# A macaron transformer block on one core: new order around the projections, five score banks at the end, seven row maxima a head taken by way of ScalarE and GpSimd

## The chip, the cores and the metric

The kernel runs on one core of one Trainium2 chip. The metric is the device time of one launch in microseconds (us), the median of the runs. Engines are named as the profile names them: PE is TensorE (matmuls), PEld its weight loads, DVE is VectorE, ACT is ScalarE, POOL is GpSimd, SP is SyncE (here it only issues DMAs). Each engine works through its own list in order and waits on semaphores for the others.

## The reference

Input x is 4096 tokens by 256 features. The block is feed-forward, attention, feed-forward:

```
x = x + 0.5 * ffn(layernorm(x))
x = x + attn(layernorm(x))
x = x + 0.5 * ffn(layernorm(x))

ffn(x):  h = x @ W_exp + b_exp ; h = butterfly(h, up) ; h = gelu(h + up_bias)
         h = butterfly(h, down) ; y = h @ W_con + b_con + down_bias
attn(x): 16 heads of 16 features, causal
         Q, K, V = x @ WQ, x @ WK, x @ WV
         probs = softmax(where(causal, Q K^T / sqrt(16), -inf))
         sum over heads of (probs @ V) @ WO
```

Everything is float32. The two butterflies are linear, so the kernel folds them into the two weight matrices once at the start.

## The kernel before

**Stages.** The start folds the weights (to about 77 us of the span). Then a loop over t = 0 to 8 runs the first feed-forward on tile t (512 tokens) and, beside it, the Q, K and V projections of tile t-1 (77 to 368 us). Then the attention runs head by head (368 to 1716 us), and at last the second feed-forward with the output projection (1716 to 1930 us).

**The loop over t.** For each tile PE runs eight hidden blocks h0 to h7 (6 matmuls each, `up_block`, L1119), of which `H_AHEAD` = 6 stand ahead of the four Q/K projections (`qk` w = 0 to 3, 6 matmuls each, L1222). The transposes of the normalized tile t-1 (XN2A, in OA) stand before block `H_AHEAD - 2`, so after four blocks. After h7 come the transposes of XN (tile t+1), the V projection (L1143) and four y blocks (L1149). Hidden blocks and qk blocks alternate over two PSUM banks (`TURNS`), so each waits until the block two places before it has been read out: `gelu_done` by ACT for h, `parts_done` for qk (ACT copies the high part, L684, DVE subtracts for the low part, `low_parts`, L935). SP stores each of the four parts to DRAM (L476), w = 0, 1 being q and w = 2, 3 being k, and loads head 0's slices back (`load_q` L437/L438, `load_k` L430/L431). DVE adds the residual of each y block (L923), takes its statistics (L774), and after the last one computes 1/sigma (L795 to L813) and normalizes into XN2A (L827). Beside the y blocks PE already computes scores for the first row maxima of head 0 (L1169) and DVE reduces them (L955 with a causal mask, L959 without); the list for block b is `beside_y`, and the ones of the last block stand on DVE before its residual.

**Attention.** The softmax needs its row maxima before the exponentials. So each score matrix is computed twice. One pass has queries on the partitions: 128 queries by 512 keys per unit (`maximum`, L1169 on PE), whose row maximum DVE takes straight from PSUM (L959, 512 elements; L955 on the diagonal). The other has keys on the partitions (`scores`, L1277), from which ACT makes exponentials (L729) into one of 8 buffers, POOL zeroes the causal triangle (L587), and PE multiplies with V (`values`, L1293). The maximum of each row is subtracted in the second pass by two extra rows of the operands (`split_step` L906 to L915 and `load_m` L449).

A head has 144 units (`UNITS`: 36 pairs (j, c) of query tile j and key tile c, times 4 blocks), in the order j = 5, 4, 3, 2, 1, 0, 6, 7. Work is issued in groups of 3 units: on PE three pairs "scores(u), maximum(u + 92)" and then the values of earlier units. The maxima run 92 units (`MX_AHEAD`) ahead of the scores. In the last head the maxima end 92 units before the scores do (`MX_UNITS` = 2212 of 2304 units); from there scores run alone. PSUM has 3 banks for scores (`S_BANKS`), so scores(u) wait for the exponential of u-3; 4 banks for maxima (`MAX_BANKS`), so maximum(u) waits until DVE has reduced u-4; one bank for the sums of values. The two score passes use different row halves of the PE array and run beside each other.

In the last head, groups 24, 25, 26 and 28 carry one output-projection block each, and group 37 the transposes of the second feed-forward's first tile.

The order of all engines is written out by hand in program order; nothing is scheduled by a tool.

## Time and profile before

| what | value |
|---|---|
| runs | 1930.58, 1930.83, 1930.94 us; median 1930.83 |
| profiled execution, its own time | 1931.87 us |
| its span (first to last instruction) | 1930.1 us |
| TensorE clock granted, mean | 0.996 of full speed |
| PE busy | 1884.0 us (98%) |
| DVE busy | 1653.3 us (86%) |
| ACT busy | 1374.1 us (71%) |
| POOL busy | 319.5 us (17%) |

How to read it: matmuls are pipelined and their modelled ends overlap, so PE counts as busy while one drains even if the next has not been issued; "98%" is not a full PE. The duration that a row gives for one instruction includes its latency; the distance between two in a row (the pitch) is shorter. The waits between engines tell more than the shares.

### The profile page before, as it was taken

How to read it: one execution, taken by the hardware profiler on the slowest of the kernel's cores; microseconds unless marked ns; L12 is line 12 of the kernel's file. 1: busy time of each engine (PE TensorE's matmuls, PEld its weight loads, DVE VectorE, ACT ScalarE, POOL GpSimd, SP SyncE). 2: the span in 40 equal slices, each digit the busy share in tenths (PEclk: the TensorE clock that was granted, in tenths of full speed). 3: DMA queues.
4: the chain of work that ended last, by engine and by line, in shares of the span. 5: the costliest groups of instructions: out<-in, count | busy, mean ns of one | idle time of the engine just before them, and what ended most of it. 6: DMA issues, size and time to landing. Idle time of an engine off the chain costs nothing.

```text
span 1930.1 us, 62111 instructions
## 1 busy us (share of the span) xinstructions
PE 1884.0 (98%) x24312; PEld 1326.1 (69%) x24312; DVE 1653.3 (86%) x3631; ACT 1374.1 (71%) x2778; POOL 319.5 (17%) x738
## 2 busy tenths in 40 slices
PE   4999999999999999999999999999999999999999
PEld 3788778666666666666666666666666666679998
DVE  7746566799999999999999999999999999746763
ACT  5412222488888888888888888888888888875443
POOL 4100000011111111111111111111111111135444
PEclk8999999999999999999999999999999999999999
DMA  7111122212111111211111121211112111102210
GB/s 202 48 56 52 53 77 78 67 48 56 42 50 46 48 44 40 55 42 51 47 46 45 41 55 41 51 46 47 46 41 55 41 49 35 55 26 66 66 44 23
DMA packets 82836, 102.40 MB, mean 53 GB/s; under 512 B 16752, under 2 KB 45168, under 8 KB 82544
## 3 DMA queue, kind: packets, MB, share of 16 engines
q1 hardware_dynamic: 81920, 98.03, 18.0%
q8 instruction: 193, 3.16, 0.7%
q14 instruction: 99, 0.81, 0.1%
q10 hardware_dynamic: 624, 0.40, 0.1%
HBM read 68.46 MB, written 29.36 MB: 51 GB/s over the span
## 4 chain that ended last, share of the span: by engine, by line
PE 91%; DVE 6%; ACT 1%; issue 1%; POOL 0%; DMA 0%; ACTq 0%; POOLq 0%; DVEq 0%
PE PS L1293 31%; PE PS L1277 29%; PE PS L1169 10%; PE PS L1149 7%; PE PS L1119 6%; PE PS L1341 5%; PE PS L1222 1%; PE PS L1143 1%; PE PS L1085 1%; DVE MXP L959 1%; DVE BNS L774 1%; DVE OA L827 1%; DVE OA L935 1%; POOL QT L609 0%; DVE OA L839 0%
## 5 line engine op out<-in xcount | busy, mean ns | idle before, releaser
L729 ACT ACTIVATE PG<-PS 128x512 f32<-128x512 f32 (+3 forms) x2304 | 1137.0, 562 | 161.5 <-PE PS L1277 136.4
L959 DVE TENSOR_REDUCE MXP<-PS 128x1 f32<-128x512 f32 x1792 | 1088.2, 682 | 14.0 <-PE PS L1169 13.1
L1169 PE MATMUL PS<-KT,QT 48*128 48x512 f32 (+5 forms) x2304 | 783.1, 432 | 3.5 <-DVE MXP L959 2.2
L1277 PE MATMUL PS<-QT,KT 50*128 50x512 f32 (+3 forms) x2304 | 727.2, 421 | 0.3
L1293 PE MATMUL PS<-PG,VH 128*17 128x128 f32 x16896 | 651.1, 275 | 0.1
L1293 PEld LDWEIGHTS PS<-PG,VH 128*17 128x17 f32 x16896 | 432.7, 97 | 197.4 <-issue 181.7
L1277 PEld LDWEIGHTS PS<-QT,KT 50*128 50x128 f32 x2304 | 360.0, 184 | 267.7 <-ACT PG L729 193.9
L1169 PEld LDWEIGHTS PS<-KT,QT 48*128 48x128 f32 (+1 forms) x2304 | 371.9, 184 | 24.9 <-DVE MXP L959 13.3
L587 POOL TENSOR_SCALAR_AFFINE_SELECT PG<-PG 128x128 f32<-128x128 f32 x512 | 145.1, 292 | 964.3 <-ACT PG L729 953.9
L955 DVE CUSTOM_DVE_ANT_0 PS<-PS,MASK 128x128 f32<-128x128 f32 (+3 forms) x512 | 241.6, 514 | 38.0 <-PE PS L1169 37.3
L658 ACT ACTIVATE PG<-PS,GB 128x512 f32<-128x512 f32 x128 | 90.3, 706 | 166.4 <-PE PS L1119 166.4
L923 DVE TENSOR_TENSOR X<-PS,X 128x256 f32<-128x256 f32 x96 | 40.5, 423 | 136.8 <-PE PS L1149 91.4
L1149 PE MATMUL PS<-MD,PG 128*128 128x256 f32 x512 | 117.8, 381 | 2.2 <-DVE X L923 1.4
L1149 PEld LDWEIGHTS PS<-MD,PG 128*128 128x128 f32 x512 | 96.2, 190 | 15.9 <-DVE X L923 1.8
L1119 PE MATMUL PS<-XTH,MU 128*128 128x512 f32 x256 | 103.3, 404 | 3.4 <-DVE MUL L893 1.6
L1119 PE MATMUL PS<-XTH,MUL 128*128 128x512 f32 x256 | 100.9, 394 | 0.0
L1119 PE MATMUL PS<-XTL,MU 128*128 128x512 f32 x256 | 100.6, 393 | 0.0
L609 POOL TENSOR_TENSOR QT<-PG,KT 128x512 fp32r<-128x512 f32 x64 | 85.8, 1383 | 82.5 <-ACT PG L658 82.5
L566 POOL TENSOR_TENSOR X<-X,OB 128x1024 f32<-128x1024 f32 x16 | 38.3, 2393 | 277.5 <-DVE XN L827 251.8
L578 POOL COPY VH<-V 128x68 f32<-128x68 f32 x128 | 30.3, 240 | 270.0 <-PE PS L1293 193.5
L1341 PE MATMUL PS<-W,KT 128*128 128x256 f32 x256 | 74.1, 289 | 0.6 <-POOL QT L609 0.6
L955 DVE DVE_READ_ACCUMULATOR2_ANT MXP<- 128x1 f32 x512 | 73.6, 144 | 0.0
(113 smaller groups left out, 1209.5 us busy)
## 6 DMA issues: line engine op xcount, KB each, us to landing
QT<-q_parts SPq DMA_DIRECT2D x256, 64.0 KB
KT<-k_parts SPq DMA_DIRECT2D x256, 64.0 KB
q_parts<-OA SPq DMA_DIRECT2D x16, 512.0 KB, 2.8
QT<-q_parts SPq DMA_DIRECT2D x256, 32.0 KB
k_parts<-OA SPq DMA_DIRECT2D x16, 512.0 KB, 4.9
KT<-k_parts SPq DMA_DIRECT2D x256, 32.0 KB
o_parts<-OS SPq DMA_DIRECT2D x128, 64.0 KB
OA<-o_parts SPq DMA_DIRECT2D x32, 256.0 KB
```

The lines of the kernel that those rows point to most:

```text
L587: nc.gpsimd.affine_select(out=tri, in_=tri, compare_op=ALU.is_ge, fill=0.0, base=0, pattern=[[1, P]], channel_multiplier=-1).then_inc(mask ...
L609: nc.gpsimd.tensor_tensor(GL[:, b, :].bitcast(f32r), G[:, b, :], GH[:, b, :], ALU.subtract).then_inc(gl_rdy, 1)
L658: nc.scalar.activation(G[:, b, :], src, ACT.Gelu, bias=GB[:, b:b + 1]).then_inc(gelu_done, 1)
L729: nc.scalar.activation(PB[u % P_BUFFERS][:, q0:TILE], bank(u % S_BANKS)[:, q0:TILE], ACT.Exp, scale=1.0 / DH ** 0.5).then_inc(exp_done, 1)
L955: nc.vector.tensor_tensor_reduce(out=s, in0=s, in1=MASK[:, 3 * P - qs * P:3 * P - qs * P + w], scale=1.0, scalar=-3e38, op0=ALU.add, op1=A ...
L959: nc.vector.tensor_reduce(dst, bank(b), AX.X, ALU.max).then_inc(mx_red, 1)
L1119: last = mm(dst, w[:, k, b * P:(b + 1) * P].bitcast(f32r), x[:, k, :].bitcast(f32r), start=(k == 0 and x is XTH and w is MU), stop=(k == D ...
L1149: last = mm(y_bank(b, y), lhs[:, k, b * P:(b + 1) * P], rhs[:, k, :], start=(k == 0), stop=(k == nk - 1))
L1169: mm(bank(b, w), q[0:rows, (BT * place(j) + qs) * P:(BT * place(j) + qs + 1) * P].bitcast(f32r), k[0:rows, c * TILE:c * TILE + w].bitcast( ...
L1277: mm(bank(u % S_BANKS)[:, q0:TILE], kt[0:SM, kb * P:(kb + 1) * P].bitcast(f32r), qt[0:SM, place(j) * TILE + q0:(place(j) + 1) * TILE].bitc ...
L1293: last = mm(O_SUM[qs * Q32:qs * Q32 + DV, :], VH[:, c * BT + kb, :], PB[u % P_BUFFERS][:, qs * P:(qs + 1) * P], start=(j == c and kb == 0) ...
L1341: last = mm(y_bank(b, y), g[:, i, cols].bitcast(f32r), w[:, i, :].bitcast(f32r), start=(i == 0 and w is MDH and g is GH), stop=(i == HB - ...
```

## The change

Five edits in one:

1. `H_AHEAD` goes from 6 to 7. Seven hidden blocks stand ahead of the projections, one behind, and the transposes of XN2A stand after five blocks.
2. On DVE, of the last y block's list the items from the third on (`beside[2:]`) move behind the normalization into XN2A; `normalize(XN, t + 1)` moves ahead of `low_parts`.
3. The four parts are computed and stored in the order q low half, k low half, q high half, k high half (`PART_AT`). SP loads q for head 0 after the third store and k after the fourth, waiting for the second store instead of the third; `load_m(0)` follows the third store instead of the second.
4. From unit 2212 on, scores use five banks (`LAST_BANKS`): the three and two of the maxima's.
5. For items m of a head with m % 12 == 1 off the diagonal (seven: 13, 37, 49, 97, 109, 121, 133), from unit 36 on, ACT copies the 512 scores from PSUM to SBUF (`copy_maxima`), POOL folds the two halves of 256 into their maximum with three operations (subtract, clamp at zero, add; `fold`), and DVE reduces the 256 that are left three groups later (`final_maximum`). The count of `mx_red` no longer follows the item's number, so waits go by a table (`RED_N`).

The first place is DVE's list in the loop over t, in the iteration t = 4, from the last y block to the low parts (OA is the normalized tile t-1, X from PS are the transposed parts). Before:

```order
L959 TENSOR_REDUCE MXP<-PS 128x1 x4
L923 TENSOR_TENSOR X<-PS,X 128x256
L774 BN_STATS BNS<-X 128x6
L795 TENSOR_TENSOR LN<-BNS 128x4
...
L827 TENSOR_SCALAR OA<-X,MEAN,RSTD 128x256 x4
L867 CAST X<-PS 128x1024
L869 TENSOR_TENSOR X<-PS,X 128x1024
L935 TENSOR_TENSOR OA<-PS,OA 128x512 x4
L827 TENSOR_SCALAR XN<-X,MEAN,RSTD 128x256 x4
```

The same place after the change:

```order
L1032 TENSOR_REDUCE MXP<-PS 128x1 x2
L996 TENSOR_TENSOR X<-PS,X 128x256
L847 BN_STATS BNS<-X 128x6
L868 TENSOR_TENSOR LN<-BNS 128x4
...
L900 TENSOR_SCALAR OA<-X,MEAN,RSTD 128x256 x4
L1032 TENSOR_REDUCE MXP<-PS 128x1 x2
L940 CAST X<-PS 128x1024
L942 TENSOR_TENSOR X<-PS,X 128x1024
L900 TENSOR_SCALAR XN<-X,MEAN,RSTD 128x256 x4
L1008 TENSOR_TENSOR OA<-PS,OA 128x512 x4
```

Two reductions have moved from ahead of the residual to behind the normalization, and XN's normalization from behind the low parts to ahead of them.

The second place is SP's list at the last tile's parts (MT holds the split maxima that `load_m(0)` brings into the score operands). Before:

```order
L476 DMA q_parts<-OA 128x2x512 x2
L449 DMA QT<-MT 2x16x32 x4
L437 DMA QT<-q_parts 32x1x512
L438 DMA QT<-q_parts 16x512
L437 DMA QT<-q_parts 32x1x512
L438 DMA QT<-q_parts 16x512
L476 DMA k_parts<-OA 128x2x512 x2
```

After:

```order
L508 DMA q_parts<-OA 128x2x512
L508 DMA k_parts<-OA 128x2x512
L508 DMA q_parts<-OA 128x2x512
L480 DMA QT<-MT 2x16x32 x4
L468 DMA QT<-q_parts 32x1x512
```

The four small loads from MT now stand behind three stores, not two.

The third place is ACT's list in a head, around its diagonal pair (5, 5) (PG from PS are exponentials, OS the sums of values). Before:

```order
L729 ACTIVATE PG<-PS 128x384
L729 ACTIVATE PG<-PS 128x256
L738 ACTIVATE OS<-PS 128x128
L729 ACTIVATE PG<-PS 128x128
L729 ACTIVATE PG<-PS 128x512 x21
```

After:

```order
L788 ACTIVATE PG<-PS 128x384
L788 ACTIVATE PG<-PS 128x256
L808 ACTIVATE OS<-PS 128x128
L788 ACTIVATE PG<-PS 128x128
L788 ACTIVATE PG<-PS 128x512 x2
L800 ACTIVATE OA<-PS 128x512
L788 ACTIVATE PG<-PS 128x512 x12
L800 ACTIVATE OA<-PS 128x512
L788 ACTIVATE PG<-PS 128x512 x7
```

A copy of 512 (OA from PS) now stands among the exponentials once every 12 units.

The diff, cut to its core:

```diff
+PART_AT = (0, 2, 1, 3)
+FINAL_BEHIND = 3
+C_BUFFERS = 6
+FOLD_WIDTHS = (256,)
+FOLD_STEPS = 3 * len(FOLD_WIDTHS) - 1
-H_AHEAD = 6
+H_AHEAD = 7
+COPIED = frozenset(m for m in range(NU) if m % 12 == 1)
...
+        def copied(u):
+            _, _, j, c, _ = unit(max_item(u))
+            return NU // 4 <= u < MX_UNITS and j != c and max_item(u) % NU in COPIED
+        def finals_in(g):
+            return [u for u in items_in(g - FINAL_BEHIND) if copied(u)] if g >= FINAL_BEHIND else []
+        LAST_BANKS = [(MX_UNITS + i) % S_BANKS for i in range(S_BANKS)] + [MAX_BANKS[3], MAX_BANKS[2]]
+        def s_bank(u):
+            return u % S_BANKS if u < MX_UNITS else LAST_BANKS[(u - MX_UNITS) % len(LAST_BANKS)]
...
             for t in range(NT):
+                for w in range(3):
+                    store_part(t, w)
+                if t == NT - 1:
+                    load_m(0)
...
+                sp.wait_ge(parts_out[0], 16 * (t + 2))
+                load_q(NQ, 0, t, ld_nq[t])
+                load_q(CQ, 0, t, ld_cq[t])
+                store_part(t, 3)
+                sp.wait_ge(parts_out[1], 16 * (t + 2))
                 load_k(NK, 0, t, ld_nk[t])
                 load_k(CK, 0, t, ld_ck[t])
...
+            def fold(u):
+                n = COPY_N[u]
+                c = COPY[n % C_BUFFERS]
+                pool.wait_ge(mx_copied, n + 1)
...
+                    nc.gpsimd.tensor_tensor(d, d, c[:, 0:w], ALU.subtract).then_inc(fold_step, 1)
+                    pool.wait_ge(fold_step, done + 1)
+                    nc.gpsimd.tensor_scalar(d, d, 0.0, None, ALU.max).then_inc(fold_step, 1)
+                    pool.wait_ge(fold_step, done + 2)
+                    last = nc.gpsimd.tensor_tensor(c[:, 0:w], d, c[:, 0:w], ALU.add)
...
+                last.then_inc(mx_folded, 1)
             for g in range(GROUP_N):
                 for u in group_units(g):
                     mask(u)
+                for u in items_in(g):
+                    if copied(u):
+                        fold(u)
...
+            def copy_maxima(u):
...
+                if n >= C_BUFFERS:
+                    act.wait_ge(mx_red, RED_N[COPIES[n - C_BUFFERS]])
+                act.wait_ge(mx_ps, max_item(u) + 1)
+                nc.scalar.activation(COPY[n % C_BUFFERS], bank(mx_bank(u)), ACT.Copy).then_inc(mx_copied, 1)
...
                     normalize(XN2A, t - 1, seq_p(t - 2) + 1 if t > 1 else None)
+                    for item in beside[2:]:
+                        maximum0(*item)
...
+                if t + 1 < NT:
+                    normalize(XN, t + 1, seq_f(t) + 1)
                 if t:
                     low_parts(t - 1, pair(late, "qk") if t < NT else ())
-                if t + 1 < NT:
-                    normalize(XN, t + 1, seq_f(t) + 1)
...
+                        beside = beside_y(late, soon, t, b)
+                        residual_block(t, t, b, beside[:2] if b == BT - 1 else beside)
...
+            def final_maximum(u):
+                _, n, j, c, qs = unit(max_item(u))
+                dve.wait_ge(mx_folded, COPY_N[u] + 1)
+                nc.vector.tensor_reduce(MXP[...], COPY[...][:, 0:FOLD_WIDTHS[-1]], AX.X, ALU.max).then_inc(mx_red, 1)
             for g in range(GROUP_N):
+                for u in finals_in(g):
+                    final_maximum(u)
...
+                elif before >= 0 and copied(before):
+                    pe.wait_ge(mx_copied, COPY_N[before] + 1)
...
-                if u >= S_BANKS:
+                if u == MX_UNITS + S_BANKS:
+                    pe.wait_ge(mx_red, H * NMX + FREE_MX)
+                elif u >= MX_UNITS + len(LAST_BANKS):
+                    pe.wait_ge(exp_done, u - len(LAST_BANKS) + 1)
+                elif u >= S_BANKS and s_bank(u) < S_BANKS:
                     pe.wait_ge(exp_done, u - S_BANKS + 1)
```

## Rows read from the trace of the kernel before

**Rows 1.** Busy time in one stretch of the attention; columns: stretch, length, each engine (instructions).
```profile
800.00:1000.00 200.00, 200.00 (x3194) 128.58 (x3192) 197.06 (x435) 173.72 (x362) 25.15 (x92) 1.00 0.18 47
```
**Rows 2.** The chain in order of time: start, length, what; one piece per head.
```profile
1109.84 1.22 PE PS L1293 x28
1278.03 1.22 PE PS L1293 x28
```
**Rows 3.** Groups by line, whole trace: busy us, mean ns | idle before, releaser.
```profile
L959 DVE TENSOR_REDUCE MXP<-PS 128x1 f32<-128x512 f32 x1792 | 1088.2, 682 | 14.0 <-PE PS L1169 13.1
L906 DVE TENSOR_REDUCE NEGM<-MXP 128x16 f32<-128x128 f32 x32 | 9.0, 281 | 0.1
L684 ACT ACTIVATE OA<-PS 128x512 fp32r<-128x512 f32 x32 | 19.1, 598 | 33.9 <-PE PS L1222 33.9
L587 POOL TENSOR_SCALAR_AFFINE_SELECT PG<-PG 128x128 f32<-128x128 f32 x512 | 145.1, 292 | 964.3 <-ACT PG L729 953.9 <-issue 0.6
L314 POOL TENSOR_TENSOR V<-V 128x256 f32<-128x256 f32 x1 | 0.7, 724 | 0.1
```
**Rows 4.** Timelines of attention: DVE, then PE's value phases and ACT without DVE's wait.
```profile
1039.81 10.85 DVE L959 TENSOR_REDUCE MXP<-PS 128x1 f32<-128x512 f32 x18
1101.48 0.85 PE L1293 MATMUL PS<-PG,VH 128*17 128x128 f32 x24
1104.92 0.85 PE L1293 MATMUL PS<-PG,VH 128*17 128x128 f32 x24
1102.86 3.25 ACT L729 ACTIVATE PG<-PS 128x512 f32<-128x512 f32 x6 [0.17 <-PE PS L1277]
```
**Rows 5.** Who waited for whom, whole trace: total us, times, longest.
```profile
PEld PS L1085 <- DVE OA L827: 11.8, 8, 1.7
PEld PS L1119 <- DVE OA L935: 4.8, 14, 0.5
PEld PS L1169 <- issue: 3.0, 5, 1.1
```
**Rows 6.** Timelines of DVE and PE at t = 4, and PE at t = 8.
```profile
187.68 1.29 DVE L959 TENSOR_REDUCE MXP<-PS 128x1 f32<-128x512 f32 x2 [0.90 <-PE PS L1169]
193.24 1.38 DVE L827 TENSOR_SCALAR OA<-X,MEAN,RSTD 128x256 f32<-128x256 f32 x4 [0.15 <-DVE RSTD L813]
194.67 1.09 PE L1085 MATMUL PS<-ident,OA 128*128 128x128 f32 x8 [1.31 <-DVE OA L827]
352.71 1.09 PE L1085 MATMUL PS<-ident,OA 128*128 128x128 f32 x8 [1.47 <-DVE OA L827]
```
**Rows 7.** The chain in order of time at t = 3: two hidden blocks.
```profile
155.46 2.75 PE PS L1119 x12
```
**Rows 8.** Timelines of SP and PE at t = 4: k loads and first maxima.
```profile
206.94 0.93 SPq L476 DMA_DIRECT2D k_parts<-OA  x2
211.64 0.61 SPq L430 DMA_DIRECT2D KT<-k_parts  x1
217.35 0.47 PE L1169 MATMUL PS<-KT,QT 128*128 128x128 f32 x2 [0.68 <-issue]
```
**Rows 9.** Timelines of SP, DVE and PE where the attention begins.
```profile
363.56 2.66 SPq L449 DMA_DIRECT2D QT<-MT  x4
364.21 0.69 DVE L935 TENSOR_TENSOR OA<-PS,OA 128x512 fp32r<-128x512 f32 x1 [1.09 <-ACT OA L684]
367.67 0.49 PE L1277 MATMUL PS<-QT,KT 50*128 50x512 f32 x1
```
**Rows 10.** Timelines of PE and ACT in the last head, scores alone.
```profile
1706.28 1.25 PE L1277 MATMUL PS<-QT,KT 50*128 50x512 f32 x3
1708.24 0.76 PE L1277 MATMUL PS<-QT,KT 50*128 50x512 f32 x3
1709.71 1.25 PE L1277 MATMUL PS<-QT,KT 50*128 50x512 f32 x3
1708.84 3.05 ACT L729 ACTIVATE PG<-PS 128x512 f32<-128x512 f32 x6 [0.39 <-PE PS L1277]
```

More of the change, by code:

```diff
@@ L187, in wide @@
             return oa[:, i * DK * TILE:(i + 1) * DK * TILE].rearrange("p (k t) -> p k t", k=DK)
+        COPY = [oa[:, 5 * DK * TILE + i * TILE:5 * DK * TILE + (i + 1) * TILE] for i in range(C_BUFFERS)]
         OT, SUMS, XT2B = [wide(i) for i in range(2)], [wide(2 + i) for i in range(2)], wide(4)
@@ L375, in max_item, with items_in @@
             return u + MX_AHEAD
+        def copied(u):
+            _, _, j, c, _ = unit(max_item(u))
+            return NU // 4 <= u < MX_UNITS and j != c and max_item(u) % NU in COPIED
+        def items_in(g):
+            return [u for u in group_units(g) if u < MX_UNITS]
+        def finals_in(g):
+            return [u for u in items_in(g - FINAL_BEHIND) if copied(u)] if g >= FINAL_BEHIND else []
+        COPY_N = {u: n for n, u in enumerate(u for u in range(MX_UNITS) if copied(u))}
+        COPIES = list(COPY_N)
+        RED_N = {}
+        for g in range(GROUP_N):
+            for u in finals_in(g) + [u for u in items_in(g) if not copied(u)]:
+                RED_N[u] = MX_AHEAD + FREE_MX + len(RED_N) + 1
         def split_items(i):
@@ L708, in _ @@
                     mix_a_side(1, (2,), range(4, 8))
+                    gelus(0, 0, range(6, H_AHEAD))
                 elif t < NT:
@@ L742, in _ @@
                     exponential(u)
+                for u in items_in(g):
+                    if copied(u):
+                        copy_maxima(u)
                 for u in VALUES_IN[g]:
@@ L1215, in _ @@
                         turn_free("qk", u)
-                        cols = slice((w % 2) * P, (w % 2 + 1) * P)
+                        part = PART_AT[w]
+                        cols = slice((part % 2) * P, (part % 2 + 1) * P)
                         for k in range(DK):
@@ L1219, in _ @@
                                 pe.wait_ge(xt_rdy, seq_p(t - 1) + 1)
-                            high, low = WH[:, w // 2, k, cols], WL[:, w // 2, k, cols]
+                            high, low = WH[:, part // 2, k, cols], WL[:, part // 2, k, cols]
                             for i, (wt, x) in enumerate(((high, X2H), (high, X2L), (low, X2H))):
```

49 lines of the change are left out of this document (28 added, 21 removed).

## The prediction

> **What bounds the kernel now.** I read four views. The page's busy shares first: they name PE (98%), but a draining matmul counts as busy, so they don't decide. Then the busy time per stretch: in 200 us of attention DVE works 197.1 us, ACT 173.7, POOL 25.2 [rows 1]. The groups by line say the same: DVE waited only 14.0 us in front of its 1792 reductions of 512 scores [rows 3]. So from 368 to 1660 us DVE is the tightest engine. The chain gives the period of a head, (1278.03 - 1109.84) / 2 = 84.10 us [rows 2], that is 1.75 us for each of 48 groups of three units.
>
> Then the timelines. DVE takes 18 reductions in 10.85 us; without the last one's tail that is 0.598 us each, 1.79 us for three [rows 4]. Where DVE is ahead (after diagonal maxima, which are cheaper), PE's value phases start at 1101.48 and, two groups on, at 1104.92, which is 1.72 us a group [rows 4]. This is a ring: scores(u) wait for the exponential of u-3, and ACT makes six in 3.25 us and waits again [rows 4]. Its own pitch is about 0.49 us (six in 3.05 less a tail of 0.1) [rows 10], so of 3.44 us ACT has 0.48 idle, 0.24 a group. So DVE's bound is above the ring's by only 0.07 us a group. That is the number that limits what the maxima edit can bring.
>
> In the loop over t the waits are PE's: 11.8 us for the normalized tile before the transposes, 8 times; 4.8 us for low parts before hidden blocks, 14 times; 3.0 us of "issue" before first maxima, 5 times [rows 5]. In the last head alone PE goes in pairs of groups, 1706.28 to 1709.71, 3.43 us for six units, while ACT needs 2.95 [rows 10].
>
> **The loop over t: the wait before the transposes.** At t = 4 two reductions take DVE 1.2 us ahead of the last residual, and the normalization ends at 194.62, after which PE starts, having idled 1.31 us, up to 1.7 in its weight queue [rows 5, 6]. The edit takes the 1.2 us out of this chain and puts one more hidden block in front of the transposes; two blocks last 2.75 us, one 1.38 [rows 7]. Together 2.6 us against at most 1.7: the wait goes. Up to t = 3 the last y block has no third item, and the block alone does it, save some 0.2 at t = 1. The wait at t = 8 (1.47, about 1.7 in the queue) stays, for no block is there to fill it [rows 6]. So 11.8 - 1.7 - 0.2 = 9.9 us. What is late next: the moved reductions start where the transposes are still running, and the cast needs these, so they hide; after the transposes two blocks follow as before, so the first projection finds its operands as early as now.
>
> **Normalizing XN earlier** puts 1.4 us of DVE in front of the low parts. DVE idles there, since ACT has to read out a projection that PE has yet to run (before the third low part of the last tile it idles 1.09 us [rows 9]). I cost it at nothing; without cover it would be up to 1.4 us for seven tiles, 10 us.
>
> **One hidden block behind the projections instead of two.** Of the 14 waits for low parts the longest is 0.5; if h6's seven are all that long, 1.3 us is left for h7's seven, 0.17 each [rows 5]. h7 now waits for the third, and the smaller wait goes: 7 x 0.17 = 1.2 us of the 4.8.
>
> **Order of the parts.** At t = 4 the third and fourth part's stores are issued from 206.94 on, k's loads only at 211.64, when the third has landed, and PE stands at 217.35 for them [rows 8]. Now the k half that head 0 needs is stored second, so it has landed by the time of the fourth store, and its loads follow that one at about 208, 3.5 us earlier, against maxima that come 1.4 us earlier. So the 3.0 us of "issue" go [rows 5].
>
> **Against it: the first scores.** `load_m(0)` stood behind the second store and was issued from 363.56 to 366.22; the first scores start at 367.67 without a wait in PE's row, so at most 1.4 us after the last load's issue. The third low part ends at 364.90, and with its store's issue (0.4) ahead the loads now start at about 365.3, 1.8 us later [rows 9]. A landing of 1.2 us leaves 0.2 to 0.3 in hand, so the first scores start some 1.5 us later, once (bounds 0.4 and 1.8).
>
> Sum of the stage: -9.9 - 1.2 - 3.0 + 1.5 = -12.6 us. Ends: -14 and, with the normalization uncovered and the last wait doubled, -1.
>
> **Five banks in the last head.** ACT's rhythm there has 0.39 us idle per six exponentials, and PE's phase of three scores lasts 1.2 us when it waits for an exponential and 0.7 when it doesn't (group periods 1.96 and 1.47) [rows 10]. With five banks scores run two further ahead and the long phase goes: the floor is PE's 1.47 or ACT's 3 x 0.49 = 1.48 us a group instead of 1.72. 31 groups, of which some 24 full: 12 pairs x 0.47 = 5.6 us. Off goes about 1 us: the wait for the last reduction before the first borrowed bank, and the last split's loads, which are on time by under 1 us now and will be overtaken. So -4.6; ends -5.7 and -1.5.
>
> **The seven maxima a head.** There are 4 in the first head, 7 in each of 14, 4 in the last: 106. DVE: a reduction of 128 has a mean of 281 ns, one of 512 of 682 [rows 3], so one of 256 is 281 + 401/3 = 415 ns, and each copied item frees 682 - 415 = 267 ns. 106 x 0.267 = 28.3 us is the most that the edit can give. ACT: a copy of 512 from PSUM has a mean of 598 ns [rows 3], a pitch of 0.49 like the exponentials. It stands behind the third exponential of a group, where 0.24 us is idle on average; 0.25 is pushed into the next group. In four of the seven places that group's first exponential is the 128-wide one of a diagonal, some 0.23 us shorter, which leaves hardly anything. So of twelve units: DVE 12 x 0.598 = 7.18 before, 6.91 after; the ring 4 x 1.72 = 6.88 plus 0.02 in four places and about 0.22 in three. The larger counts: gains of 0.25 in four places and 0.08 in three, 1.24 us a head. One of the three (item 49, issued beside unit 101) lies in a stretch where PE already runs at the ring's pace: nothing to gain, 0.1 to 0.2 to lose. That leaves 1.1 us a head, 1.1 x 106/7 = -16.7 us. Ends: -28.3, and +26 if each copy pushed the ring by the full 0.25 and DVE's relief bought nothing.
>
> POOL: three operations of 256. A two-input one takes 724 ns, the one-input one at least what 128 columns of the causal mask take, 292, and at most 724 [rows 3]: 1.74 to 2.17 us, plus waits between them, about 2.2. Masks queue behind it on POOL, and the values wait for them; but after each copied unit the next diagonal unit is at least three units away, and the values of that one are a group behind. DVE asks for the folded half three groups later. From the third exponential of the group to there are 7 units of 0.58 plus DVE's lag of about 0.5, so 4.6 us, less 1.1 for the copy: 3.5 us for a fold of 2.2. Hidden.
>
> A page speaks against folding on POOL. The masked reductions (PSUM and one SBUF input) and the plain ones are as long beside a mask on POOL as without, which is what the near-constant 0.598 says [rows 4]. "SBUF — State Buffer" of the Trainium skill (section "SBUF: two separate sides") states that a VectorE operation with two SBUF inputs, or one in a two-port mode, and a GpSimd operation lock each other out for a whole instruction. By that rule only the casts and subtractions of the splits could collide, and they stand in other groups than the folds: the sum stays, and only if the lock reached further is there the rival E. No run here yet shows a fold.
>
> **Sum.** -12.6 - 4.6 - 16.7 = -33.9 us, from the profiled execution's 1931.9 (span 1930.1, 1.8 around it): 1898.0. That execution is 1.0 above the median of the runs, so 1897. The second feed-forward is untouched.
>
> **Rivals.**
> A, the forecast: 1897, by itself 1890 to 1905. Chance 0.55.
> B, the ring takes all of DVE's relief: ACT's copies cost what they free. For it speaks the margin of 0.07 us a group; against it the four places beside a short exponential. 1930.8 - 12.6 - 4.6 = 1914. Chance 0.17.
> C, the ring has more give than its unhindered pace shows, and all 28.3 us come: 1885. For it: DVE's waits for PE are small everywhere. Chance 0.12.
> D, the stage keeps its waits, moved to the low parts behind the early normalization or to the y blocks: only a few us of 12.6: about 1907. The three waits were all short and late in a chain, which speaks against it. Chance 0.08.
> E, DVE's reduction of the fold, or a masked one beside it, is blocked for the length of a POOL operation, 0.72: 0.2 to 0.3 us for each of 106, 1920 to 1925. Chance 0.03.
> F, slower: ACT is late for the ring after every copy. Its price is 0.25 x 106 = +26.5, less 17.2 from the other two parts: 1940. It turns the sign from 0.16 us net loss per copied item on. Against it: only every fourth group has a copy, and ACT has 0.48 us idle in two. A fold longer than 3.5 us would do the same by way of DVE. Chance 0.05.
>
> The range 1883 to 1916 holds A, B, C and D but for their edges. What a measurement of this kernel can tell from no change is 0.2%, 3.9 us: all but F is faster by more, so faster 0.93, within 0.2% 0.02, slower 0.05.
>
> **What the profile after would show.** PE's wait for the normalized tile at 1.7 us in all instead of 11.8, "issue" before the first maxima gone, periods of t shorter by 1 to 2.5 us, the first scores waiting for loads after the V projection. Heads of about 83.0 us instead of 84.1; DVE's idle time in the attention up, from 3 us in 200 to 4 or more; the reductions of 256 near 415 ns; POOL some 230 us more busy; ACT at 90% instead of 87. The last 92 units in about 50 us instead of 55. Wrong would be: heads at 84 us or more with PE's scores waiting for exponentials after copies (B, F), DVE idle in front of the folded reductions (F's second way), waits in front of the low parts (D).

## The result, and the profile of the changed kernel

| | before | after |
|---|---|---|
| median of the runs, us | 1930.88 (1930.58 to 1932.65, 4 runs) | 1913.53 (1912.39 to 1914.80, 4 runs) |
| ratio | | 0.9906, 95% interval 0.9893 to 0.9918 |
| profiled execution / span, us | 1931.9 / 1930.1 | 1913.25 / 1911.5 |

The kernel is 17.4 us faster by the medians. The forecast was 1897. Sign and range held; the size is half of what was worked out. Cut at the same events in both traces, the spans differ by 18.6 us:

| stretch | before, us | after, us | change | forecast |
|---|---|---|---|---|
| start to the first set of XN2A transposes (t = 1) | 78.46 | 76.66 | -1.8 | the stage as a whole: -12.6 |
| from there to the set at t = 8 | 274.25 | 263.92 | -10.3 | |
| from there to the first exponential | 15.49 | 17.04 | +1.5 | |
| head 0 | 83.92 | 85.82 | +1.9 | -0.6 |
| heads 1 to 14, mean of one | 84.13 | 83.82 | -0.31, in all -4.4 | -1.1, in all -15.4 |
| head 15 up to unit 2212 | 30.49 | 30.04 | -0.4 | -0.6 |
| last 92 units | 54.87 | 49.78 | -5.1 | -4.6 |
| rest | 214.76 | 214.78 | 0 | 0 |

The forecast of the profiled execution was 1898.0 and it took 1913.25. Of these 15.3 us the heads from 1 on hold 11.2, head 0 holds 2.5 and the stage 2.0; the last 92 units came out 0.5 better than forecast.

The first row is not the work of the change. The first set of transposes starts at 76.7 to 80.2 us in the eleven kernels of this document that have the stage as it is after the change, the changed kernel among them, and the scatter is there before the loop over t begins. The second row is: 263.9 to 266.5 us in the same eleven, 7.8 to 10.3 below the kernel before.

**The stage.** The waits of the kernel after, as in [rows 5] (engine and line, who was waited for: total us, times, longest; L1170 is L1085 of before, L1204 is L1119, L1254 is L1169):

```profile
PEld PS L1204 <- DVE OA L1008: 3.6, 7, 0.5
PEld PS L1170 <- DVE OA L900: 2.0, 2, 1.7
PEld PS L1254 <- issue: 1.1, 2, 0.7
```

11.8 us of waits for the normalized tile are 2.0, of which 1.7 is the one at t = 8; the seven short waits for low parts are gone, 1.2 us; of the 3.0 us of "issue" 1.1 are left in this execution. These are waits of PE's weight queue, and what they cost is less. At t = 4 before the change, where PE's row shows 1.31 us idle [rows 6], the queue waited 1.73, but from the start of the last matmul ahead to the first transpose it took 1.70 us where 0.23 is the distance without a wait:

```profile
192.97 0.39 PE L1119 MATMUL PS<-XTH,MUL 128*128 128x512 f32 x1
194.67 0.86 PEld L1085 LDWEIGHTS PS<-ident,OA 128*128 128x128 f32 x8 [1.73 <-DVE OA L827]
```

Over t = 1 to 7 these distances sum to 9.9 us before and 1.6 after, so the wait's going gave 8.3 us, not 9.8. At t = 4 the two timelines of [rows 6] are now these (start, length, what):

```profile
186.37 1.38 DVE L900 TENSOR_SCALAR OA<-X,MEAN,RSTD 128x256 f32<-128x256 f32 x4 [0.15 <-DVE RSTD L886]
187.67 1.28 DVE L1032 TENSOR_REDUCE MXP<-PS 128x1 f32<-128x512 f32 x2
```
```profile
188.90 0.39 PE L1204 MATMUL PS<-XTH,MUL 128*128 128x512 f32 x1
189.13 1.03 PE L1170 MATMUL PS<-ident,OA 128*128 128x128 f32 x8
```

The tile is ready at 187.67 and PE reaches its transposes at 189.13 without a wait: 1.4 us in hand. The last k part and its loads come in one go now. Before, the first of them was issued at 211.64 [rows 8], 4.2 us after the transposes of XN had started (207.48); here those start at 200.51, and the load follows 2.0 us later:

```profile
201.96 0.52 SPq L508 DMA_DIRECT2D k_parts<-OA  x1
202.52 0.61 SPq L461 DMA_DIRECT2D KT<-k_parts  x1
```

**The first scores, and what they brought with them.** SP, then PE, where the attention begins, against [rows 9]:

```profile
352.78 0.36 SPq L508 DMA_DIRECT2D q_parts<-OA  x1
353.19 2.65 SPq L480 DMA_DIRECT2D QT<-MT  x4
```
```profile
354.73 0.87 PE L1228 MATMUL PS<-W,X 128*128 128x256 f32 x6
357.12 0.46 PE L1369 MATMUL PS<-QT,KT 50*128 50x512 f32 x1 [1.52 <-DMA QT<-MT]
```

PE stands 1.5 us for the loads of the maxima, which are issued behind the third store; their last issue ends at 355.84 and the scores start 1.28 us later. That was the forecast. What was not: PE had been busy up to that gap, and from 358.2 us on the granted clock is down at the lower level (columns: PE, PEld, DVE, ACT, POOL busy, then PEclk, DMA share, GB/s):

```profile
354.00:358.00 4.00, 2.48 (x20) 1.94 (x18) 0.66 (x3) 1.54 (x4) 1.49 (x8) 1.00 0.34 115
358.00:365.00 7.00, 6.81 (x53) 3.92 (x54) 5.22 (x9) 3.71 (x9) 1.10 (x4) 0.51 0.42 126
365.00:372.00 7.00, 7.00 (x125) 4.35 (x122) 6.86 (x13) 6.30 (x12) 0.00 (x0) 1.00 0.35 74
```

0.51 is the 1.2 GHz level, for nearly the whole of 7 us in which PE is busy for 6.81. The kernel with the loads early, below, has neither the gap nor this stretch, and not head 0's +1.9 us either.

**The heads.** The chain in order of time, one piece a head, of which two ten heads apart stand here (start, length, what), and the busy time of the stretch that [rows 1] shows for before:

```profile
679.60 1.22 PE PS L1385 x28
1517.67 1.22 PE PS L1385 x28
```
```profile
800.00:1000.00 200.00, 200.00 (x3198) 128.02 (x3194) 195.45 (x437) 181.50 (x383) 64.81 (x150) 1.00 0.18 48
```

(1517.67 - 679.60) / 10 = 83.81 us a head. ACT has risen from 173.7 to 181.5 us of 200, POOL from 25 to 65, DVE has fallen only from 197.1 to 195.5. The groups by line (busy us, mean ns | idle before):

```profile
L1032 DVE TENSOR_REDUCE MXP<-PS 128x1 f32<-128x512 f32 x1686 | 1041.5, 681 | 23.7 <-PE PS L1254 16.8
L637 POOL TENSOR_SCALAR OA<-OA 128x256 f32<-128x256 f32 x106 | 89.5, 845 | 9.3
L635 POOL TENSOR_TENSOR OA<-OA 128x256 f32<-128x256 f32 x106 | 77.6, 732 | 290.9 <-ACT OA L800 290.9
L639 POOL TENSOR_TENSOR OA<-OA 128x256 f32<-128x256 f32 x106 | 77.5, 731 | 8.8
L800 ACT ACTIVATE OA<-PS 128x512 f32<-128x512 f32 x106 | 64.7, 611 | 0.0
L1102 DVE TENSOR_REDUCE MXP<-OA 128x1 f32<-128x256 f32 x106 | 43.4, 409 | 0.0
```

The reduction of a folded half takes 409 ns (forecast 415), the copy 611 (598), so each copied item does free 0.27 us of DVE and costs ACT no more than was put down. DVE never waits for a folded half (idle 0.0 before L1102). What DVE got, it idles away in part. The 14.0 us in front of the plain reductions before [rows 3] and the 23.7 now are of the whole trace, and 13.8 and 12.2 of them lie in the loop over t; from 372 to 1640 us, in the attention, it is 0.2 us before and 11.4 now. In heads 1 to 14 together DVE's idle time has risen from 19.3 to 31.7 us, and they are 4.4 us shorter. The unit prices were right, and the worth of a freed 0.27 us was not.

**The last head.** ACT in [rows 10] idled 0.39 us per six exponentials. Now, in the head's last stretch of scores:

```profile
1684.87 11.87 ACT L788 ACTIVATE PG<-PS 128x512 f32<-128x512 f32 x24 [0.39 <-PE PS L1369]
```

24 exponentials in 11.87 us without a gap among them: 0.49 us each, which is ACT's own pitch.

### The profile page after: what moved, and what is told of

It reads as the page before. It is cut to its first block, busy times and chain, and to the rows that moved or that the text cites. A ratio compares the mean times of both kernels' runs of the same rounds, so it can differ in the third digit from the quotient of the medians.

```text
span 1911.5 us, 62638 instructions
## 1 busy us (share of the span) xinstructions
PE 1869.8 (98%) x24312; PEld 1310.3 (69%) x24312; DVE 1634.6 (86%) x3631; ACT 1416.7 (74%) x2884; POOL 562.6 (29%) x1056
## 4 chain that ended last, share of the span: by engine, by line
PE 94%; DVE 3%; ACT 1%; DMA 1%; POOL 0%; issue 0%; SPq 0%; POOLq 0%; ACTq 0%; DVEq 0%
PE PS L1385 31%; PE PS L1369 30%; PE PS L1254 9%; PE PS L1204 8%; PE PS L1234 7%; PE PS L1433 5%; PE PS L1310 1%; PE PS L1170 1%; PE PS L1228 1%; DVE OA L1008 1%; DMA PG<-w_exp_t 1%; ACT OA L698 0%; POOL QT L667 0%; DVE OA L912 0%; ACT OA L742 0%
## 5 line engine op out<-in xcount | busy, mean ns | idle before, releaser
L1032 DVE TENSOR_REDUCE MXP<-PS 128x1 f32<-128x512 f32 x1686 | 1041.5, 681 | 23.7 <-PE PS L1254 16.8
L1254 PE MATMUL PS<-KT,QT 48*128 48x512 f32 (+5 forms) x2304 | 782.6, 430 | 2.7 <-DVE MXP L1032 2.2
L1254 PEld LDWEIGHTS PS<-KT,QT 48*128 48x128 f32 (+1 forms) x2304 | 373.9, 185 | 22.4 <-DVE MXP L1032 8.9
L635 POOL TENSOR_TENSOR OA<-OA 128x256 f32<-128x256 f32 x106 | 77.6, 732 | 290.9 <-ACT OA L800 290.9
L667 POOL TENSOR_TENSOR QT<-PG,KT 128x512 fp32r<-128x512 f32 x64 | 85.8, 1382 | 80.7 <-ACT PG L716 80.7
L1204 PE MATMUL PS<-XTH,MU 128*128 128x512 f32 x256 | 102.2, 399 | 3.5 <-DVE MUL L966 1.6
L1204 PE MATMUL PS<-XTH,MUL 128*128 128x512 f32 x256 | 100.0, 391 | 0.0
L1204 PE MATMUL PS<-XTL,MU 128*128 128x512 f32 x256 | 99.8, 390 | 0.0
L637 POOL TENSOR_SCALAR OA<-OA 128x256 f32<-128x256 f32 x106 | 89.5, 845 | 9.3
```

Source lines behind the costliest of these rows:

```text
L637: nc.gpsimd.tensor_scalar(d, d, 0.0, None, ALU.max).then_inc(fold_step, 1)
L1032: nc.vector.tensor_reduce(dst, bank(b), AX.X, ALU.max).then_inc(mx_red, 1)
L1204: last = mm(dst, w[:, k, b * P:(b + 1) * P].bitcast(f32r), x[:, k, :].bitcast(f32r), start=(k == 0 and x is XTH and w is MU), stop=(k == D ...
L1254: mm(bank(b, w), q[0:rows, (BT * place(j) + qs) * P:(BT * place(j) + qs + 1) * P].bitcast(f32r), k[0:rows, c * TILE:c * TILE + w].bitcast( ...
```

## The experiments

Twelve kernels ran, each timed in several rounds beside the kernel before on the same chip. Ratios are to the kernel before, with 95% intervals. "Head" is the mean of heads 1 to 14, from the exponentials' starts in the profile. Where it matters, units are counted within a head (0 to 143), as are the items of the maxima.

### No copies

```diff
-COPIED = frozenset(m for m in range(NU) if m % 12 == 1)
+COPIED = frozenset()
```

> The changed kernel with no item copied: all maxima are reduced by VectorE from PSUM, the rest of the change stays. What the copies are worth by themselves, all else equal. Theory R (the ring of scores and exponentials over three banks sets the pace of the attention almost everywhere, so VectorE's relief turns into idle time): heads back at 84.08 us, time 1913.5 + 4.8 = 1918. Theory of the prediction (1.1 us a head): 1930. A theory S (the copies cost as much as they bring, and the small gain per head comes from elsewhere): 1913 to 1915.

Measured: 1921.53 us (1918.94 to 1923.24), ratio 0.9946 (0.9931 to 0.9961). Head 84.19 us, last 92 units 49.65. So five banks give their 5 us without any copy, the heads without copies are those of before, and seven copies are worth 84.19 - 83.82 = 0.37 us a head. The medians of the two kernels differ by 8.0 us, their profiles by 8.6, but 3.9 of those lie ahead of the attention, where nothing was edited; so the worth of the copies is read from the heads here, and from the heads below.

### Half reductions: VectorE relieved as far as it goes

No copies, and each unmasked reduction in the attention reads 256 of its 512 scores (half of the keys are left out of those maxima).

```diff
-nc.vector.tensor_reduce(dst, bank(b), AX.X, ALU.max)
+nc.vector.tensor_reduce(dst, bank(b)[:, 0:256], AX.X, ALU.max)
```

> No item copied, and every unmasked row maximum takes only the first 256 of its 512 columns (the other half of the keys is left out of the maxima). VectorE is freed of 0.27 us in each of 112 units a head, 30 us a head, and ScalarE and GpSimd have nothing added: this shows the pace of the ring without VectorE and without copies. Theory R: heads of about 82.5 to 83.3 us, barely under the changed kernel's 83.75, time 1900 to 1910. If VectorE were the bound and only ScalarE's copies had eaten the gain: heads under 82 us, time under 1890.

Measured: 1889.61 us (1889.07 to 1890.56), ratio 0.9782 (0.9768 to 0.9797); head 82.27 us. The group and the stretch:

```profile
L1032 DVE TENSOR_REDUCE MXP<-PS 128x1 f32<-128x256 f32 x1792 | 658.2, 418 | 321.0 <-PE PS L1254 320.6
```
```profile
800.00:1000.00 200.00, 200.00 (x3270) 124.61 (x3268) 137.41 (x449) 177.83 (x371) 26.69 (x97) 1.00 0.18 46
```

DVE idles 321 us in front of its reductions, and a head is only 1.92 us shorter than with none of this. That is about all that relief of DVE can bring here: 15 heads x 1.9 = 29 us for some 60 us of idle DVE in each 200. The forecast's pace of the ring, 1.72 us for each of 48 groups, makes 82.56 us and was nearly right (82.27). So the ring was sized well; how fast one gets down to it was not.

### Copies without their use

Seven copies a head of the same size on ScalarE, read from SBUF; nothing is folded and DVE reduces every item from PSUM.

```diff
-nc.scalar.activation(COPY[n % C_BUFFERS], bank(mx_bank(u)), ACT.Copy).then_inc(mx_copied, 1)
+nc.scalar.activation(COPY[n % C_BUFFERS], MD[:, 0:2, :].rearrange("p a b -> p (a b)"), ACT.Copy).then_inc(mx_copied, 1)
...
-                for u in finals_in(g):
-                    final_maximum(u)
-                    if u < MX_UNITS and not copied(u):
+                    if u < MX_UNITS:
```

> Nothing is copied from the maxima, VectorE reduces all of them from PSUM and GpSimd folds none, but ScalarE makes a copy of 512 (from the folded down weights in SBUF into a spare buffer) at the same 106 places. ScalarE's burden without any relief. Theory R says that ScalarE is in the ring: each copy costs 0.02 to 0.25 us, 0.5 to 1 us a head on top of 84.1, against the kernel without copies +7 to +15 us. If ScalarE's idle time swallows the copies: within 2 us of the kernel without copies, about 1918.

Measured: 1924.07 us (1923.01 to 1926.35), ratio 0.9962 (0.9948 to 0.9976); head 84.41. Copies alone cost 0.22 us a head. That is not 0.03 each: units 100 to 107, where item 49 is copied, take 4.91 us here and 4.67 without copies, so this one copy costs 0.24, the 0.25 that rival F needed, and the other six together nothing (beside the copy of item 133 units 40 to 43 are 0.17 us longer, and 44 to 47 give 0.15 back). With the relief they are 0.37 ahead of none, so the relief, with the other release of the copied items' banks, is worth 0.59 us of the 7 x 0.27 = 1.87 that it frees.

### No fold

POOL folds nothing; DVE reduces the first 256 of the copy (half of the keys of the copied items are left out).

```diff
-                    if copied(u):
-                        fold(u)
...
-                dve.wait_ge(mx_folded, COPY_N[u] + 1)
+                dve.wait_ge(mx_copied, COPY_N[u] + 1)
```

> The changed kernel, but GpSimd folds nothing: VectorE reduces the first 256 columns of the copy as soon as ScalarE has made it (the other half of those keys is left out of these 106 maxima). GpSimd's part alone is taken away. Theory R: no difference, 1912 to 1914. If the fold of 2.5 us (its clamp takes 845 ns and not the 292 to 724 that were assumed) held up masks or VectorE's last reduction: faster by up to 0.2 us a copy, 1895 to 1908.

Measured: 1914.36 us (1913.72 to 1914.87), ratio 0.9910 (0.9895 to 0.9925); head 83.84 against 83.82. The fold, 732 + 845 + 731 ns on POOL, is hidden to the last tenth, and nothing on DVE is shorter for its absence (L1102 has 409 ns in both). Rival E is out, and F by way of late folds.

### The maxima's loads back behind the second store

```diff
 for w in range(3):
     store_part(t, w)
-if t == NT - 1:
-    load_m(0)
+    if t == NT - 1 and w == 1:
+        load_m(0)
```

> The changed kernel with the first loads of the split maxima back behind the second store. In the changed kernel PE waits 1.7 us in front of the first scores, and its granted clock is then at the lower level from 358 to 365 us of the span. Theory: the wait goes, and with it the stretch at the lower clock, which costs head 0 some 1.9 us: 1913.5 - 3.4 = 1910. If the stretch at the lower clock has nothing to do with the wait: only 1.5 us, 1912.

Measured: 1911.41 us (1909.69 to 1913.60), ratio 0.9900 (0.9885 to 0.9914): 2.1 us below the kernel after in another set of runs, with intervals that overlap, so the times alone don't carry it. The profiles do: head 0 takes 83.58 us instead of 85.82, and PE has the full clock in the stretch where it had half:

```profile
354.00:358.00 4.00, 4.00 (x22) 3.42 (x23) 1.66 (x3) 1.99 (x4) 0.00 (x0) 1.00 0.71 264
358.00:365.00 7.00, 6.74 (x72) 4.89 (x72) 5.03 (x10) 5.13 (x13) 2.48 (x12) 1.00 0.56 178
```

Over all profiles: the five with three score banks and the loads behind the third store have 3.4 or 6.8 us of low clock just behind the first scores, the seven with the loads behind the second (before among them) have none after the first exponential. In full-reduction kernels head 0 then takes 84.9 to 86.0 us in the one case (84.9 and 85.1 behind 3.4 us, 85.8 and 86.0 behind 6.8) and 83.4 to 83.9 in the other. A piece of 3.4 us at the lower level 11 to 13 us ahead of the first exponential is another matter: nine of the fourteen kernels have it, the one before the change too, with and without the gap.

### The same, and item 49 not copied

```diff
-COPIED = frozenset(m for m in range(NU) if m % 12 == 1)
+COPIED = frozenset(m for m in range(NU) if m % 12 == 1 and m not in (49,))
```

> As the kernel before it (loads early), and item 49 of a head is no longer copied, so six instead of seven a head. Theory R: at that place ScalarE's copy pushes the ring and VectorE's relief buys nothing (the pairs (6, 2) and (6, 1) are 0.23 + 0.04 us longer than before the change, 0.07 comes back at (6, 0)): 0.2 us a head less, 15 times, 1907. If each copy is worth the same seventh of the gain: +0.7, 1911.

Measured: 1907.38 us (1906.82 to 1908.79), ratio 0.9880 (0.9863 to 0.9896), the shortest of all with the whole computation. Head 83.57 against 83.84 with seven: the seventh copy costs 0.27 us a head where the forecast had put a loss of 0.1 to 0.2. It is the sharpest sign that a copy's worth is a matter of its place, and the kernel with copies alone shows what this one costs: units 100 to 107 take 4.90 us with all seven, 4.91 with copies alone, 4.69 here and 4.67 without any. ScalarE's time is lost there and DVE's relief brings nothing.

### Four score banks, three for the maxima

With copies and without, loads early in both; the last 92 units keep five banks.

```diff
-S_BANKS = 3
+S_BANKS = 4
-MAX_BANKS = (4, 5, 7, 3)
+MAX_BANKS = (4, 5, 7)
```

> Loads early, all seven copies, and one PSUM bank moved from the maxima (three left) to the scores (four) for the whole attention. Scores of u then wait for the exponential of u-4. Theory R: the ring over three banks is what limits, so four free it, and VectorE, with its relief, becomes the bound: heads of about 82.5, time 1890 to 1900. If the fourth bank of the maxima is what keeps VectorE fed: PE waits for VectorE more, heads of 84 to 86, time 1915 to 1940.

> As the kernel with four score banks, without any copy. Theory R: VectorE is then the bound in nearly every group, 83.0 us of work a head plus some waits, about the same as now, 84: time 1912 to 1918, so that the copies are worth 10 to 20 us in this form where they are worth under 5 in the other. If the number of score banks does not matter: the difference between the two stays under 5.

Measured: 2022.74 us, ratio 1.0475 (1.0459 to 1.0490), head 91.08 with copies; 2004.83 us, 1.0385 (1.0369 to 1.0400), head 89.91 without. So the score ring doesn't set the pace by itself: a bank added there and taken from the maxima costs 6 to 7 us a head. The waits of PE for the maxima's banks, without copies, show why (49 waits with 13.3 us of before, whole trace, have become these):

```profile
PEld PS L1254 <- DVE MXP L1032: 101.0, 369, 2.7
```

PE takes scores and maxima in one order, so a maxima bank that isn't free holds up the scores as well. And here seven copies lose 1.17 us a head, relief and all, where with four maxima banks they win 0.37. A copied item keeps its bank until ACT comes to it, and the trace with copies shows PE waiting for that, in each of heads 1 to 14 once, behind item 49's place, for 0.47 us (whole trace):

```profile
PEld PS L1254 <- ACT OA L800: 7.7, 17, 0.7
```

That is 0.47 of the 1.17 us; the rest is not accounted for.

### One copy a head, item 133

Loads early.

```diff
+COPIED = frozenset((133,))
```

> load_m(0) early, and of the seven maxima a head only item 133 (beside the scores of unit 41) is copied, folded and taken from SBUF. Theory of places: relief of VectorE counts only where the ring stands behind VectorE, and of the seven that is the stretch of units 48 to 51 after item 133 (2.70 to 2.39 us there, 0.31 a head), so one copy keeps nearly all: heads 1 to 14 take 83.85 to 83.95 us each (83.57 with six copies, 84.19 with none), the kernel 1909 to 1915. Theory of sums (each copy gives its share of one pool of VectorE time): a sixth of the gain is left, 84.08 a head, the kernel about 1917.

Measured: 1910.62 us (1909.58 to 1912.11), ratio 0.9895 (0.9881 to 0.9908); head 83.87. One copy of seven gives 0.32 of the 0.37 us that the seven give, as the theory of places said; a share of a common pool would have left 0.1. It gives half of the 0.62 that the six without item 49 give. The gain lies in units 48 to 51 alone, 2.69 us with no copy, 2.39 here. ACT there, first without copies, then with this one (start, length, what, idle before):

```profile
811.48 1.57 ACT L788 ACTIVATE PG<-PS 128x512 f32<-128x512 f32 x3 [0.18 <-PE PS L1369]
813.72 1.57 ACT L788 ACTIVATE PG<-PS 128x512 f32<-128x512 f32 x3 [0.66 <-PE PS L1369]
```
```profile
805.01 1.57 ACT L788 ACTIVATE PG<-PS 128x512 f32<-128x512 f32 x3 [0.18 <-PE PS L1369]
806.90 1.09 ACT L788 ACTIVATE PG<-PS 128x512 f32<-128x512 f32 x2 [0.32 <-PE PS L1369]
```

What ACT waits for begins at DVE. In the kernel without copies PE's weight queue stands there for a maxima bank that DVE has not reduced; the values follow at 812.13, the scores behind them at 813.13:

```profile
811.70 0.18 PEld L1254 LDWEIGHTS PS<-KT,QT 48*128 48x128 f32 x1 [0.28 <-DVE MXP L1032]
```

Such waits are rare. In heads 1 to 14 together the kernel before and this one have:

```profile
PEld PS L1169 <- DVE MXP L959: 9.3, 43, 0.3
```
```profile
PEld PS L1254 <- DVE MXP L1032: 5.2, 28, 0.3
```

Before, they stand at three places a head, beside units 48 (0.28 us), 63 and 75 (0.18 each). With the one copy the first is gone and the other two are left. So at this place DVE's backlog stalls the ring once a head, 0.66 us of waiting for scores in ACT's row, and 0.34 of it goes with one relief a few units ahead. Elsewhere DVE is just as busy, but PE hardly ever stands for it.

### Five other places

Loads early; items 133, 4, 13, 76 and 101.

```diff
+COPIED = frozenset((4, 13, 76, 101, 133))
```

> load_m(0) early, and five other maxima a head copied: items 133 (unit 41), 4 (56), 13 (65), 76 (128), 101 (9), where the run with half reductions showed the units behind them shorter (by 0.18 at units 60 to 63, 0.16 at 68 to 71, 0.19 at 132 to 135, 0.12 at 8 to 15). Theory of places: these five give 0.31 + about 0.10 to 0.15 each, less five copies of ScalarE at 0.03: heads of 83.2 to 83.5, the kernel 1901 to 1907, the shortest of all. Theory of sums: five copies are worth five sixths of six: 83.67 a head, the kernel 1909. If other places only shift the waits on, 83.8 or more.

Measured: 1916.58 us (1914.69 to 1917.04), ratio 0.9923 (0.9911 to 0.9936); head 84.21. A miss for both numbers: the places that gain under full relief don't gain under one copy each. Item 4 gives 0.07 us (units 60 to 63), and item 76 nothing (units 132 to 135: +0.08). Units 8 to 15 lose 0.56, less 0.15 behind them, and there is a wait that no other kernel with four maxima banks has:

```profile
PEld PS L1254 <- ACT OA L800: 9.3, 15, 0.8
```

15 waits in 15 heads, all at the same place. ACT and PE, one of them (start, length, what, idle before):

```profile
782.95 1.58 ACT L788 ACTIVATE PG<-PS 128x512 f32<-128x512 f32 x3
784.40 0.62 ACT L800 ACTIVATE OA<-PS 128x512 f32<-128x512 f32 x1
784.88 1.61 ACT L788 ACTIVATE PG<-PS 128x512 f32<-128x512 f32 x3
787.10 1.09 ACT L788 ACTIVATE PG<-PS 128x512 f32<-128x512 f32 x2 [0.61 <-PE PS L1369]
```
```profile
784.50 0.39 PE L1369 MATMUL PS<-QT,KT 50*128 50x512 f32 x1
785.07 0.50 PE L1254 MATMUL PS<-KT,QT 48*128 48x512 f32 x1 [0.18 <-ACT OA L800]
```

This is the second way of a copy's cost, one that the forecast didn't have: a copied item's bank comes free when ACT has copied it, behind the third exponential of its group, not when DVE has reduced it. Where DVE isn't late the copy frees the bank later than DVE would have (the kernel without copies has no wait at this place). PE stands for it (0.6 us in its weight queue), scores stand behind that, and ACT idles 0.61 us three exponentials on.

### The stage's two covers, one at a time

Both start from the kernel with loads early and item 49 not copied (1907.38). In the first, the two maxima go back ahead of the normalization of XN2A:

```diff
-                    for item in beside[2:]:
-                        maximum0(*item)
...
-                        residual_block(t, t, b, beside[:2] if b == BT - 1 else beside)
+                        residual_block(t, t, b, beside)
```

> The kernel with six copies (without item 49) and load_m(0) early, with the two maxima of beside[2:] back in front of the normalization of XN2A. The prediction's step: TensorE again waits for VectorE ahead of each set of transposes of XN2A, 1.4 us at each of seven tiles: the stretch from the first to the eighth set grows by 9 to 10 us, the kernel takes 1916 to 1918 against 1907.4. Rival: the new order of XN and of the stores took those waits off, and the stretch grows by less than 3 us: 1908 to 1911.

In the second, `H_AHEAD` goes back from 7 to 6.

> The same kernel with six copies, with H_AHEAD = 6: ScalarE takes six gelus, not seven, ahead of the high parts. The prediction's step: TensorE waits for the bank of the seventh hidden block again, 0.17 us at each of seven tiles: 1.2 us more, 1908.6. Rival: high parts one gelu earlier give back as much on the way to the projections: 1906 to 1908; the other side: the first exponential comes later by over 3 us, if the projected parts then stand behind more maxima.

Measured: 1908.28 us (1907.50 to 1909.04), ratio 0.9882 (0.9868 to 0.9895), and 1909.11 us (1907.51 to 1910.00), ratio 0.9883 (0.9868 to 0.9899). The stretch from the first to the eighth set of transposes is 264.73 us in the kernel that they start from, 265.73 and 266.26 in these. Neither difference can be leaned on: kernels with the same stage scatter over 263.9 to 266.5, and with `H_AHEAD` at 6 the first seven sets stand a block of 1.4 us earlier against the eighth, which makes the stretch longer without costing anything. The waits are steadier. What PE's weight queue waits there for the normalized tile, first and second:

```profile
PEld PS L1168 <- DVE OA L900: 3.5, 6, 1.7
```
```profile
PEld PS L1170 <- DVE OA L900: 6.2, 8, 1.7
```

The text expected 9 to 10 us of the first edit alone. That was wrong, and against the forecast's own arithmetic, by which the wait is covered twice: by 1.4 us of one more hidden block and, from t = 4 on, by 1.2 us of moved maxima. In PE's weight queue before the change the waits at t = 1 to 7 were 1.62, 0.81, 0.77, and four times 1.73. With the block alone (first kernel) they are 0.26, 0, 0, and four times about 0.39; with the moved maxima alone (second) 1.64, 0.81, 0.79, and four times about 0.31; with both, 0.28 and then none. So from t = 4 on each edit alone takes 1.35 to 1.4 of 1.73 and both together the rest, and up to t = 3 only the block counts. This is the forecast's split, tile by tile. In the queue the pair takes 9.8 us, the block alone 8.3 and the moved maxima alone 5.6; in distances between the starts of PE's matmuls 8.3, 7.8 and 5.6. So leaving out the moved maxima costs 0.5 us and leaving out the block 2.6; the times of the two kernels, 0.9 and 1.7 us over 1907.38 with ranges that overlap, are too close to show it. The waits for low parts rise in the second kernel from 3.6 us in 7 to 4.3 in 11, so four of the seven short ones come back, 0.7 us of the 1.2 that were expected.

## Why the forecast was right in sign and wrong in size

**Loop over t.** Right by its steps, with one size wrong and one step not borne out. Waits for the normalized tile are down by 9.8 (forecast 9.9) and those for low parts by 1.2 (1.2), but the forecast took waits of the weight queue for time, and in starts of matmuls the first term is 8.3. The 3.0 us of "issue" were to go; here 1.1 are left, but the other ten kernels with the same stage show 1.1 to 4.0 us, two of them more than the kernel before, so this one figure can't be leaned on. The k loads do come 2.1 us earlier against what PE does, as worked out (3.5, less the 1.4 by which PE is earlier itself); that it took any of the "issue" off is not shown. Up to the eighth set of transposes the forecast was -14.1 us; the loop gave 7.8 to 10.3, and the -12.1 of the profile has 1.8 in it from ahead of the loop, which is luck. The early normalization of XN cost nothing that can be seen: the waits for low parts fell. The order of the loads cost the 1.5 us that were put down, and 2 us more in head 0, by the clock behind the gap, for which the forecast had no term; the loads are best behind the second store, with the order of the parts as it is.

**Five banks.** Right: -4.6 forecast, -5.1 measured, by the mechanism named (ACT's gaps go).

**Seven maxima: the step that failed.** "The larger counts: gains of 0.25 in four places and 0.08 in three, 1.24 us a head." The prices under it held: reduction 409 ns for 415, copy 611 for 598, fold hidden, ring's floor 82.3 us a head for 82.6. What didn't hold is that a head's time is the larger of two averages over twelve units. It would be if every stretch were behind DVE by the same amount. By the forecast's own figures the whole way from a head to the ring's pace was 84.1 - 82.6 = 1.5 us, and seven copies among 112 reductions were to take 1.1 of it. In fact PE stands for DVE at three places a head, 0.64 us in all, and longest at one (0.28 us, with 0.66 us of ACT's waiting in units 48 to 51); a copy shortly ahead of that one takes 0.32 us. The other six together add 0.05: the five that remain without item 49 add 0.30, in steps of up to 0.11 over several stretches, and item 49 takes 0.27 back, more than the 0.1 to 0.2 that was put down for it. The net is 0.31 against before and 0.37 against no copies, where 1.1 was forecast: 11.2 of the 15.3 us by which the profiled execution missed. Head 0 with its clock is 2.5 more, the stage up to the first exponential (10.6 for 12.6) another 2.

**The rivals.** The time is B's, 1914, but only by accident of sums. By B the copies would give nothing; they give 0.37 us a head, and B's 1914 has the whole stage in it, of which 2 us, and 2 more in head 0, did not come. C needed heads of 84.13 - 1.89 = 82.2 us from seven copies. The half reductions do reach that, 82.27, but with 30 us of relief a head and DVE idle a third of the time; from 1.87 us of relief came 0.37. D falls by the waits. E falls by the kernel without a fold: with 106 folds beside them DVE's plain reductions have a mean of 681 ns, before it was 682 [rows 3]. The Trainium skill ("SBUF — State Buffer", section "SBUF: two separate sides") confines the lock between VectorE and GpSimd to VectorE's operations with two SBUF inputs or in a two-port mode; the plain reduction reads one PSUM bank and is not one of these, and the trace agrees. F is right at one of the seven places and wrong at six: the copy of item 49 costs 0.24 us by itself, the 0.25 of the rival, and the others nothing in the sum. At unit 9 a copy costs some 0.4 us a head, but by a bank held, not by the exponentials that the rival spoke of.

**What stays open.** Why DVE's backlog reaches PE just beside units 48, 63 and 75; and how the 1.92 us between 84.19 and 82.27 could be had. It is three times the 0.64 that PE waits for DVE, and relief ahead of four further places that shorten under full relief gave next to none of it, so it is not a sum of local gains of one copy each. The trace shows where waits end, not which earlier delay they carry. Whether a copy set ahead of its group's exponentials, which would free the bank earlier, does better was not tried.

## What to carry to other kernels

Where an engine is 98% busy and a ring of buffers beside it has 2% to spare (82.3 of 84.1 us), don't take the larger of the two averages as the period: look, stretch by stretch, for the places where the feeding engine really stands for the busy one (here PE for DVE, three a head, the largest with a gap of 0.66 us in ACT's row behind it), and relieve the busy engine just ahead of them. Then take the helpers out one at a time: one copy did nine tenths of the work of seven, and half of the work of six, because the seventh lost 0.27 us of what the others had gained. A buffer handed to a second engine comes free by that engine's queue, so price the later release as well as the work. And when a load is moved, price the gap that it opens on TensorE twice, for its length and for what the clock may take behind it.

## What the runs showed of the hardware

- A stall of 1.2 to 1.5 us on a busy TensorE as the attention begins was followed, in each of the five kernels that had it, by 3.4 or 6.8 us at the 1.2 GHz level, and by none in the seven with three score banks that didn't have it; head 0 was 1.4 to 2.5 us longer for it. The length of the stall doesn't tell the length of the fall: 1.17 and 1.54 us came before 3.4, and 1.51 and 1.52 before 6.8. The two kernels with four score banks had 3.4 us at that level there with the loads early, so the stall isn't the only way to it.
- The one-input `tensor_scalar` maximum on POOL, 128x256 in float32, took 845 ns; the two-input `tensor_tensor` of that size 732. The forecast had taken a two-input operation as the upper bound of a one-input one.
- On DVE a reduction of 256 scores has a mean of 409 ns from SBUF and 418 from PSUM, one of 512 from PSUM 681; 106 folds on POOL beside them changed neither the 409 nor the 681 (409 without folds, 682 before); the 418 was measured without folds only.
